# Attention products in 64-row halves of TensorE's array, two PSUM banks for each result, and whole-image group sums

## The reference

```python
def _forward(x, Wq, Wk, Wv, Wo, bo, pos_emb, scale):
    xh = x.transpose(0, 2, 3, 1)
    q, k, v = xh @ Wq, xh @ Wk, xh @ Wv
    q2, k2, v2 = (win(q), win(k), win(v))      # b, 64 places, heads, 16 windows, 28
    q2 = q2 * scale
    sim = jnp.einsum('bmhid,bmhjd->bmhij', q2, k2) + pos_emb
    attn = jax.nn.softmax(sim, axis=-1)
    o = jnp.einsum('bmhij,bmhjd->bmhid', attn, v2)
    ...
    return (o @ Wo + bo) ...
x = x + _forward(_gn(x), ...)
```

## Time and profile before

| | us |
|---|---|
| median of three runs | 3929.71 |
| the profiled execution, its own time | 3934.19 |
| its span, first to last instruction | 3932.4 |
| TensorE busy | 3778.8 |
| VectorE busy | 3103.2 |
| ScalarE busy | 2733.0 |
| GpSimd busy | 2014.2 |

### The profile page before, as it was taken

One profiled execution on the slowest core, in us unless ns is written; L12 is line 12 of the kernel. 1 busy time (PEld: TensorE's weight loads), 2 busy tenths in 40 slices (PEclk: granted clock), 3 DMA queues, 4 the chain that ended last, 5 costly groups with the idle time before them and its releaser, 6 DMA issues.

```text
span 3932.4 us, 134126 instructions
## 1 busy us (share of the span) xinstructions
PE 3778.8 (96%) x51712; PEld 2812.8 (72%) x51712; DVE 3103.2 (79%) x5528; ACT 2733.0 (70%) x5124; POOL 2014.2 (51%) x3207
## 2 busy tenths in 40 slices
PE   4999999999999999999999999999999999999998
PEld 3777777777777777777777777777777777777776
DVE  6887878777778878787878877887788777787876
ACT  5776767767676767677776767676767767676774
POOL 4555555545555555555545555555555545555553
PEclk9999999999999999999999999999999999999999
DMA  3554555455555554555555545554555455545544
GB/s 86 131 136 125 135 133 137 126 130 138 134 126 131 142 133 125 130 143 131 128 136 131 134 125 136 134 134 125 136 134 134 127 130 139 133 126 134 141 120 113
DMA packets 248095, 513.40 MB, mean 131 GB/s; under 512 B 58576, under 2 KB 59024, under 8 KB 247440
## 3 DMA queue, kind: packets, MB, share of 16 engines
q1 hardware_dynamic: 247440, 504.40, 50.4%
HBM read 118.31 MB, written 117.44 MB: 60 GB/s over the span
## 4 chain that ended last, share of the span: by engine, by line
PE 78%; DVE 14%; issue 7%; DVEq 0%; SPq 0%; ACT 0%; POOL 0%; DMA 0%; POOLq 0%
PE ps_out L305 21%; PE ps_q L305 13%; PE ps_k L305 13%; PE ps_v L305 11%; PE ps_s L334 10%; PE ps_o L346 9%; DVE half_var L531 6%; DVE sc L581 2%; DVE var L529 2%; DVE x_sb L564 2%; PE ps_tot L393 1%; DVE var L527 1%; DVEq L183 0%; DVE pt_f L594 0%; DVE st L523 0%
## 5 line engine op out<-in xcount | busy, mean ns | idle before, releaser
L648 POOL TENSOR_TENSOR sc<-sc,mx 128x512 f32<-128x512 f32 x512 | 536.5, 1048 | 1044.1 <-DVE mx L588 1044.1
L429 ACT ACTIVATE xn<-x_sb,norm_add,norm_mul 112x128 f32<-112x128 f32 x2048 | 1033.0, 611 | 5.8 <-POOL norm_add L641 5.8
L660 POOL TENSOR_TENSOR sc<-sc,rs 128x512 f32<-128x512 f32 x512 | 537.1, 1049 | 704.4 <-DVE rs L609 700.7
L446 ACT ACTIVATE q_sb<-ps_q 128x512 f32<-128x512 f32 x512 | 305.6, 597 | 846.0 <-PE ps_q L305 845.9
L305 PE MATMUL ps_out<-ohi,wo_s 128*112 128x256 f32 x4096 | 783.7, 293 | 50.1 <-DVE x_sb L564 50.1
L305 PEld LDWEIGHTS ps_out<-ohi,wo_s 128*112 128x112 f32 x4096 | 561.6, 175 | 160.3 <-issue 82.0
L305 PE MATMUL ps_q<-xhi,wqk 112*128 112x512 f16 x2048 | 616.1, 383 | 52.6 <-issue 42.9
L576 DVE TENSOR_TENSOR olo<-ps_o,ohi 128x512 fp32r<-128x512 f32 x512 | 344.7, 673 | 370.0 <-ACT ohi L469 302.6
L305 PE MATMUL ps_k<-xhi,wqk 112*128 112x512 f16 x2048 | 610.5, 380 | 0.0
L334 PEld LDWEIGHTS ps_s<-k_bd,q_sb 128*32 128x32 f32 x16384 | 416.0, 109 | 216.2 <-issue 215.9
L305 PE MATMUL ps_v<-wv_s,xhi 112*128 112x224 f16 x4096 | 563.1, 260 | 0.0
(11 more groups left out here) (67 smaller groups left out, 5661.3 us busy)
## 6 DMA issues: line engine op xcount, KB each, us to landing
k_bd<-k_cut SPq DMA_DIRECT2D x1024, 128.0 KB, 3.3
p_bd<-pt_f SPq DMA_DIRECT2D x2048, 64.0 KB, 2.1
x_sb<-in_x SPq DMA_DIRECT2D x128, 896.0 KB, 6.0
out_y<-x_sb SPq DMA_DIRECT2D x128, 896.0 KB, 4.9
stage<-in_L_conv_Wq SPq DMA_DIRECT2D x2, 98.0 KB
stage<-in_L_conv_Wk SPq DMA_DIRECT2D x2, 98.0 KB
stage<-in_L_conv_Wv SPq DMA_DIRECT2D x2, 98.0 KB
stage<-in_L_conv_Wo SPq DMA_DIRECT2D x8, 24.5 KB
```

The costliest lines, as they stand in the source:

```text
L429: nc.scalar.activation(xn[:, b % 2, :, c4, :, :, nw].rearrange("p r c q -> p q r c"), x_sb[:, b % XBUFS].rearrange("p ch (nh r w) -> p (ch ...
L648: nc.gpsimd.tensor_tensor(rows, rows, mx[:, t % 2].unsqueeze(2).broadcast_to(by_row), ALU.subtract).then_inc(shifted, 1)
L660: nc.gpsimd.tensor_tensor(rows, rows, rs[:, t % 2].unsqueeze(2).broadcast_to(by_row), ALU.mult).then_inc(probs, 1)
```

## The change

1. `score` and `weigh_values` work in halves of 64 rows. A score product takes two heads of a group (64 rows) against 64 columns of a `k_bd` with room for two heads; a value product takes two pairs. Each product of before becomes two, one in each half of the array's rows, which write the same partitions of two different banks: `ps_s` and `ps_o` are now two banks each, one buffer each. Eight banks are in use as before.
2. Since `ps_s` has one buffer, the scores of t + 1 wait for `biased` of t. All waits of the score, the values and the totals stand before the last matmul of k (`attention_waits`).
3. The totals `ps_tot` lie in the first bank of `ps_s`, are computed between k and the scores, and by one product, since `part` now holds sums over both channel halves.
4. `group_sums` and `group_squares` reduce a whole image at once (2048 elements), at steps 2 and 3 mod 4; ScalarE squares both halves at step 2 mod 4.
5. The statistics have six operations for seven: the variance is halved from the start, the clamp adds `eps` from a tensor in a `scalar_tensor_tensor`, and the shift for the first guess stands behind both `add_out`. `st` stands behind `olo` and the wait for the scores.
6. `pos_sb` is laid out in the order of the two banks, 512 columns, and loaded by 64 transfers in place of eight.
7. `ohi` and `olo` read `ps_o` over both banks; the value product writes runs of 16.

```diff
-        k_bd = sb("k_bd", [128, 2, HG, HPG, HTOK])
+        k_bd = sb("k_bd", [128, 2, HG, 2, HTOK])
-        p_bd = sb("p_bd", [128, 2, PAIRS, UNIT * 32])
+        p_bd = sb("p_bd", [128, 2, 2, UNIT * 32])
-        ps_s = [ps(f"ps_s{n}", [128, UNIT * 32]) for n in range(2)]
-        ps_o = ps("ps_o", [128, UNIT * 32])
-        ps_tot = ps("ps_tot", [128, 2 * G])
+        ps_s = ps("ps_s", [128, 2, 512])
+        ps_o = ps("ps_o", [128, 2, 512])
+        ps_tot = ps_s[0:CP, 0, 256:256 + 2 * G]
...
-                    load_weights(pos_sb[p0:p0 + WIN, :, c2, :], pos[0, 0].rearrange("h n m -> n h m"))
-                    n_w += 1
+                    for half in range(2):
+                        for t2 in range(T2):
+                            for hg in range(HG):
+                                h = hg * HPG + half * 2
+                                load_weights(pos_sb[p0:p0 + WIN, half, t2, hg, :, c2, :],
+                                             pos[0, 0, h:h + 2].rearrange("h n m -> n h m"))
+                                n_w += 1
...
-                        col = (t2 * HG + hg) * 128
-                        for pr in range(PAIRS):
-                            tok = ((g % 2) * T2 + t2) * TILE + pr * 32
-                            last = nc.tensor.matmul(
-                                ps_s[g % 2][pr * 32:pr * 32 + 32, col:col + 128].rearrange("p (h j) -> p h j", j=32),
-                                q_sb[:, h % QBUFS, hg, tok:tok + 32],
-                                k_bd[:, h % 2, hg, :, tok:tok + 32], start=True, stop=True)
+                        col = (t2 * HG + hg) * 64
+                        for half in range(2):
+                            rows = slice(half * 64, half * 64 + 64)
+                            for pr in range(PAIRS):
+                                tok = ((g % 2) * T2 + t2) * TILE + pr * 32
+                                last = nc.tensor.matmul(
+                                    ps_s[pr * 32:pr * 32 + 32, half, col:col + 64].rearrange("p (h j) -> p h j", j=32),
+                                    q_sb[rows, h % QBUFS, hg, tok:tok + 32],
+                                    k_bd[rows, h % 2, hg, :, tok:tok + 32], start=True, stop=True)
...
+                        for half in range(2):
+                            rows = slice(half * 64, half * 64 + 64)
+                            for h in range(HPG):
+                                unit = (((h // 2) * T2 + t2) * HG + hg) * 2 + h % 2
+                                products = ps_o[h * 32:h * 32 + 32, half, :].rearrange("p (c u n) -> p c u n", c=WS // 2, n=WIN)
+                                last = nc.tensor.matmul(
+                                    products[:, :, t2 * HG + hg, :],
+                                    v_sb[rows, g % VBUFS, t2, hg * HPG + h, :],
+                                    p_bd[rows, g % 2, :, unit * 32:unit * 32 + 32], start=True, stop=True)
...
+                def attention_waits():
+                    if b is not None:
+                        per_image(pe, summed, b, i, 2)
+                    if b is not None or is_step(gs):
+                        per_step(pe, biased, t, i)
+                    if gs == 0:
+                        wait(pe, stats, STAT_OPS * 2 + 1, i, 0)
+                    if is_step(gs) and gs % 2 == 0:
+                        keys_placed(pe, gs // 2, i)
+                        per_step(pe, q_kept, gs + 1, i)
+                    if is_step(gv):
+                        probs_placed(pe, gv, i)
+                        per_step(pe, v_kept, gv, i)
+                        per_step(pe, o_lo, gv - 1, i)
...
-                    project_qk(u, 1).then_inc(k_done, 1)
+                    project_qk(u, 1, attention_waits).then_inc(k_done, 1)
+                else:
+                    attention_waits()
+                if b is not None:
+                    wait(pe, stats, STAT_OPS * (b - 1) + 1, i, STAT_OPS * XBUFS)
+                    nc.tensor.matmul(ps_tot, ones[:, :], part[:, b % 2], start=True, stop=True).then_inc(totals, 1)
...
                 square(image_at(t, SUM_LEAD), 0, i)
-                square(image_at(t, SUM_LEAD - 1), 1, i)
+                square(image_at(t, SUM_LEAD), 1, i)
...
-                    ins = nc.vector.tensor_scalar(var[:, :], var[:, :], 0.0, EPS, ALU.max, ALU.add)
-                elif n == 4:
-                    ins = nc.vector.tensor_scalar(half_var[:, :], var[:, :], 0.5, None, ALU.mult)
-                elif n == 5:
-                    ins = nc.vector.tensor_scalar(guess[:, :], var[:, :].bitcast(I32), 1, None, ALU.logical_shift_right)
+                    ins = nc.vector.scalar_tensor_tensor(half_var[:, :], half_var[:, :], 0.0, eps[:, :], ALU.max, ALU.add)
+                elif n == 4:
+                    ins = nc.vector.tensor_scalar(guess[:, :], half_var[:, :].bitcast(I32), 1, None, ALU.logical_shift_right)
...
                 add_out(t - FINAL_LAG, 0, i)
+                add_out(t - FINAL_LAG, 1, i)
                 stat_op(stat_b, 4, i)
-                add_out(t - FINAL_LAG, 1, i)
+                group_sums(image_at(t, SUM_LEAD), i)
+                group_squares(image_at(t, RSQ_LEAD), i)
                 stat_op(stat_b, 5, i)
-                group_sums(image_at(t, SUM_LEAD), 0, i)
-                group_sums(image_at(t, SUM_LEAD - 1), 1, i)
-                group_squares(image_at(t, RSQ_LEAD), 0, i)
-                group_squares(image_at(t, RSQ_LEAD - 1), 1, i)
-                stat_op(stat_b, 6, i)
```

More of the change, by code:

```diff
@@ L117, in build @@
         s_scale = sb("s_scale", [128, 1])
-        pos_sb = sb("pos_sb", [128, HEADS, 2, WIN])
+        pos_sb = sb("pos_sb", [128, 2, T2, HG, 2, 2, WIN])
         ones = sb("ones", [CP, CP])
@@ L304, in split_product @@
                     for ch in range(chunks):
+                        if waits is not None and n == 3 * chunks - 1:
+                            waits()
                         last = nc.tensor.matmul(dst, w_parts(a, ch), x_parts(c, ch),
@@ L311, in _, with project_qk @@
             o_parts = (ohi, olo)
-            def project_qk(u, j):
+            def project_qk(u, j, waits=None):
                 h, hg = divmod(u, 2)
@@ L342, in weigh_values @@
                     for hg in range(HG):
[L343 to L349 removed]
+                        for half in range(2):
[7 more added lines that the diff above has]
+                                    p_bd[rows, g % 2, :, unit * 32:unit * 32 + 32], start=True, stop=True)
                 return last
             def step(t, i):
[L353 removed]
+                u, gs, gv, b = t + PROJ_LEAD, t + 1, t - PV_LAG, image_at(t, TOT_LEAD)
+                def attention_waits():
[12 more added lines that the diff above has]
+                        per_step(pe, o_lo, gv - 1, i)
                 if is_step(u):
@@ L387, in step @@
                     last.then_inc(projected, 1)
-                b = image_at(t, TOT_LEAD)
-                if b is not None:
-                    per_image(pe, summed, b, i, 2 * CH)
-                    wait(pe, stats, STAT_OPS * (b - 1) + 1, i, STAT_OPS * XBUFS)
-                    for ch in range(CH):
-                        last = nc.tensor.matmul(ps_tot[0:CP, :], ones[:, :], part[:, b % 2, ch],
-                                                start=(ch == 0), stop=(ch == CH - 1))
-                    last.then_inc(totals, 1)
             pe.wait_ge(zeroed, N_ZEROED)
@@ L522, in stat_op @@
                 if n == 0:
-                    ins = nc.vector.tensor_scalar(st[:, :], ps_tot[0:CP, :], 1.0 / GROUP_N, None, ALU.mult)
+                    ins = nc.vector.tensor_scalar(st[:, :], ps_tot, 0.5 / GROUP_N, None, ALU.mult)
                 elif n == 1:
-                    ins = nc.vector.scalar_tensor_tensor(var[:, :], mean, -1.0, mean, ALU.mult, ALU.mult)
+                    ins = nc.vector.scalar_tensor_tensor(half_var[:, :], mean, -2.0, mean, ALU.mult, ALU.mult)
                 elif n == 2:
-                    ins = nc.vector.tensor_tensor(var[:, :], var[:, :], msq, ALU.add)
+                    ins = nc.vector.tensor_tensor(half_var[:, :], half_var[:, :], msq, ALU.add)
@@ L542, in group_sums @@
                     return
-                if ch == 0:
-                    wait(dve, x_loaded[b % XBUFS], 16 * (b // XBUFS + 1), i, 16)
-                    per_image(dve, totals, b - 2, i)
-                nc.vector.tensor_reduce(part[:, b % 2, ch, 0:G], x_sb[:, b % XBUFS, ch].rearrange(by_group, g=G, w=WW // G),
+                wait(dve, x_loaded[b % XBUFS], 16 * (b // XBUFS + 1), i, 16)
+                per_image(dve, totals, b - 2, i)
+                nc.vector.tensor_reduce(part[:, b % 2, 0:G], x_sb[:, b % XBUFS].rearrange(by_group, g=G, w=WW // G),
@@ L547, in group_sums, with group_squares @@
                                         AX.XY, ALU.add).then_inc(summed, 1)
-            def group_squares(b, ch, i):
+            def group_squares(b, i):
                 if b is None:
                     return
```

(6 more changed lines are left out.)

69 lines of the change are left out of this document (26 added, 43 removed).

## The result

The changed kernel took 4052.72 us (median of 4 runs, 4034.63 to 4059.64) beside 3930.36 us for the kernel before in the same measurement: ratio 1.0304, 95% interval 1.0269 to 1.0339. It is slower by 3.0% where 3843 us, faster, was forecast. The profiled execution took 4056.41 us, its span is 4054.6.

What follows compares the result with a forecast made beforehand. TensorE (96% busy) bounds the kernel; after the change the load loop would, at 28.9 us an image for 29.8. Rounds -90, last steps -12, early steps -8, start +24: -86 on the median gives 3843 us; range 3740 to 3960.

Steps and rivals of the forecast that it cites:

- r: Score and value products: time per matmul with its weight load; today's time, with the start's +24, reached at 14.7 ns.
- The jump: Loop's jump back: costs VectorE 3.66 us a round in the binding load loop, instead of TensorE's 2.2.
- at nothing: TensorE's clock: time added by a granted clock below full while TensorE waits was counted at nothing.
- load loop: Store, load, squares, exp: binds after the change at 28.9 us an image for 29.8, second square adding 0.95.
- Products, 0.45 us each: TensorE's score and value products: row halves overlap, 0.43 us less each, a step 6.40 us for 7.26.
- rival 1: Score and value products: halves do not overlap, TensorE keeps 7.26 us a step; 3880, up to 3915 us; chance 0.13.
- Rival 3: Score and value products: starting instructions is the bound, from just slower than today to 4810 us; chance 0.13.
- Over 1 us of room, so nothing: Waits gathered before TensorE's last k matmul: the work queued behind has over 1 us of room, so no cost.
- Whole-image sums, totals: VectorE's sums and squares counted as nothing; TensorE's totals between k and score fall from 0.34 to 0.17 us an image.
- Statistics: VectorE's statistics: the half_var stall may move to the shift; only TensorE's 0.4 us wait an image goes.
- Start: Before the loop: 64 loads of pos_sb for 8 on SyncE, all exposed, +24 us.
- Ramp and tail: Some nine steps at the start gain -8 us; the 14 last full steps, after the last load, -12 us.

Runs made afterwards that it cites:

- experiment 6: Kernel before with each score and value product cut in two by columns (64 columns, still 128 rows), so twice the instructions: 4077.84 us, ratio 1.0362.
- experiment 14: experiment 6 with a loop body ten times as long (2 rounds for 20): 3931.35 us, ratio 1.0000 to the kernel before.
- experiment 1: Changed kernel with a loop body four times as long (5 rounds for 20): 3960.65 us, ratio 1.0066 to the kernel before.
- experiment 8: Changed kernel with eight loads of the bias table and four VectorE copies in place of 64 loads: 4016.48 us, ratio 1.0222 to the kernel before.
- experiment 13: experiment 8 with a loop body ten times as long (2 rounds for 20): 3935.79 us, ratio 1.0011 to the kernel before.
- experiment 11: Changed kernel with experiment 2, experiment 7 and experiment 8 together and 2 rounds for 14: 3785.00 us, ratio 0.9618 to the kernel before.
- experiment 4: Changed kernel with SyncE issuing the four p_bd transfers ahead of the load of x: 4319.75 us, ratio 1.0981 to the kernel before.
- experiment 2: Changed kernel with ScalarE's second square of an image one step later: 4015.44 us, ratio 1.0195 to the kernel before.
- experiment 5: Changed kernel with score and value products of 128 rows and eight pos_sb loads, as in the kernel before: 3903.28 us, ratio 0.9913 to that kernel.
- experiment 12: Changed kernel with eight slots of x, loading only half of each image's channels from the ninth image on: 3875.75 us, ratio 0.9843 to the kernel before.
- experiment 7: Changed kernel with eight slots of x, the load two steps earlier and behind the p_bd transfers: 3989.19 us, ratio 1.0159 to the kernel before.

## Why the prediction was wrong, step by step

- **The step that failed: what twice the instructions cost.** The prediction priced them as starts inside a burst and asked only whether r, the time per matmul, stays under 14.7 ns. It does (10 ns). The jump stayed at 3.6 us, the clock "at nothing", and the supply of instructions had no term at all. Measured: with the doubled stream a jump costs 7.8 us (experiments 6 and 14), where it was 2.8; in the changed kernel, whose load loop uses part of the pause, 6.5 (experiment 1) or 4.2 (experiment 8 against 13: 75 us for 18). It has three parts: a longer stop at the jump, further stops right behind it, and half clock for some 3 to 7 us. And between the jumps TensorE stops inside products (experiments 1, 11 and 13) and the clock falls again, which had no term either.
- **Products, 0.45 us each.** The mechanism was right: the halves overlap, and rival 1 is out. The size was off: 0.66 us for the score, 10 ns a start for the 7 that the 0.45 us needed. A step came to 6.82 instead of 6.40 us. The floor of 25 ns a matmul (the Trainium skill, TensorE: Matmul & The Clock Gate, "Wait — 56ns, not 53.3ns?") does not hold over products on different parts of the array: 64 in 0.66 us.
- **Rival 3** had the sign and the instructions, but by its own condition (r above 14.7 ns) it would not have happened. Right side, wrong mechanism.
- **The load loop** is there. Experiment 4 shows it (squares wait 316 us more; up to +262 us), experiment 2 its second square (42 us, 0.35 an image, for the 0.95 forecast). Between jumps an image takes about 29.4 us (steps of 7.13, 6.87, 8.42 and 7.01 us, medians of the trace by their place in the image) for the 28.9 forecast.
- **"Over 1 us of room, so nothing" for the waits gathered before the last k product** was wrong: 124.6 us for `p_bd` there. The look at what is queued behind the waiting instruction stopped at TensorE; on SyncE `p_bd` stands behind the load's wait for the store, and then shares the DMA engines with it. As TensorE's steps got shorter, its need for `p_bd` came earlier, while the load loop held SyncE where it was.
- **Whole-image sums, totals**: right in sign. Between the jumps of experiment 5 the median steps of an image add up to 29.15 us for 29.77, about the 0.57 forecast, but of the 73 us (128 x 0.57) only 32 came out: its granted clock is 0.995, and it also waits 24.7 us for `p_bd` ahead of k, a wait that the kernel before does not have there.
- **Statistics**: right, the stall moved to the shift (1.38 us).
- **Start**: right. +24 forecast; the first q product stands 26.8 us later, and experiment 8 gives 25.6. **Ramp and tail**: -8 and -12 forecast, +5.0 (31.8 - 26.8) and +1.1 measured: no gain was there.

The sum: the start is 3 us over the forecast, ramp and tail missed by 13 each. The rounds missed by 179 us (+89.3 for -90). The slower pace between stops is (29.4 - 28.9) x 120 = 60 of them. The jumps, at 4.2 to 6.5 us for the 3.6 forecast, are 12 to 58 by the runs that take them away. The other 61 to 107 lie in late steps away from a jump, in which TensorE waits for `p_bd`, stops inside a product or runs at the lower clock; these overlap with the load loop, and no run parts them further. Two runs bound the whole from both sides: without the doubled instructions and their loads of `pos_sb` the change is at -32 us (experiment 5), and the doubled instructions alone are at +142 (experiment 6).

Left open: how much of a stop is the amount of other traffic and how much the distance that instructions are fetched ahead. Experiments 1 and 14 show that jumps matter, experiment 12 that traffic does; 7 and 11 change several things at once. The Trainium skill (Advanced Engine Details and Errata, "ISA Cache") says that instructions come in lines of 16 KB, 256 instructions; the 16.4 KB a packet agree. The branch of about 51 ns that the Trainium skill gives (Advanced Engine Details and Errata, "Control Flow Timing") is not what a jump costs here: 2.2 to 4.0 us.

## What to carry to other kernels

Count the instructions of the loop body before cutting products smaller. With twice the instructions each jump back cost 5.1 us more (a longer stop, stops behind it, and the lower clock after them), and a loop body four times as long took 97 us off the change's +122. When a bound engine gets faster, ask also which queue feeds it: a transfer that waits at the head of an in-order queue delays the small ones behind it, and the faster products paid only with the load two steps ahead and the long loop body together (3785 us). Look at the instruction queue when an engine stops and waits for nothing. The kernel before itself gains 1.3% from fewer jumps.

## What the runs showed of the hardware

- 64 products of 64 rows and 32 columns of weights start in 0.66 us, 10 ns for each with its weight load, and row halves overlap; the same number of columns and products on 128 rows took 1.07 us.
- A stop of 4.04 us was followed by some 3 us at the lower of the two clock levels, and so was one of 2.23 us in the kernel before. There it happened behind 5 of 19 jumps (stops of 2.0 to 2.7 us; granted clock 0.998 over the run).
- 1174 of 1193 stops of TensorE that waited for no data ended 1.0 to 2.0 us after a 16 KB packet of the instruction queue had landed.
- TensorE can stop in the middle of products that wait for no data, 7.10 us at the longest, beside a store and a load of 896 KB each; halving the load left as many stops and made them two fifths shorter.
